# Scores tiles of four heads by 32 queries, one array tile per score matmul, and another order of transfers in layer one

## What is computed

```python
# layer 0: 8 query heads of 64, one key/value head
h = rms(x) * (ln1_w * (1 + cond @ tw.T));  q, k, v = h @ Wq.T, h @ Wk.T, h @ Wv.T   # q, k rotated by position
x = x + (softmax(q @ k.T / 8) @ v) @ Wo.T
h = rms(x) * (ln2_w * (1 + cond @ tw2.T));  x = x + (silu(h @ Wg.T) * (h @ Wu.T)) @ Wd.T   # 2048 inner features
# layer 1: 16 query heads of 32, 4 key/value heads from a latent of 128
y = layernorm(x) * (1 + scale(cond)) + shift(cond)
q, k, v = y @ Wq.T, (y @ Wkd.T) @ Wku.T, (y @ Wkd.T) @ Wvu.T                        # q, k rotated
out = x + (softmax(q @ k.T / sqrt(32)) @ v) @ Wo.T
```

## Time and profile before

| | |
|---|---|
| median of 3 runs | 859.61 us (858.96 to 860.92) |
| the profiled execution | 855.91 us |
| its span, first to last instruction | 854.1 us |
| TensorE matmul busy | 834.2 us, 98% |
| TensorE weight load busy | 685.0 us, 80% |
| VectorE, ScalarE, GpSimd busy | 596.8, 442.7, 404.5 us |
| TensorE's granted clock | 1.000 of full speed |

### The profile page before, as it was taken

One profiled execution on the slowest core, in us unless ns is written; L12 is line 12 of the kernel. 1 busy time (PEld: TensorE's weight loads), 2 busy tenths in 40 slices (PEclk: granted clock), 3 DMA queues, 4 the chain that ended last, 5 costly groups with the idle time before them and its releaser, 6 DMA issues.

```text
span 854.1 us, 15629 instructions
## 1 busy us (share of the span) xinstructions
PE 834.2 (98%) x5940; PEld 685.0 (80%) x5940; DVE 596.8 (70%) x877; ACT 442.7 (52%) x819; POOL 404.5 (47%) x318
## 2 busy tenths in 40 slices
PE   9899999999999999999999999999999999999997
PEld 6687788788788788787787888887878878887885
DVE  6787466666665765766556787876867857668886
ACT  4666455455345455444447556465364454544662
POOL 2566545545544445446455646354444443531431
DMA  9902533533533533523623546446255254240001
GB/s 347 365 25 75 167 115 102 179 121 108 179 102 102 179 103 114 164 82 126 211 103 118 164 143 187 142 150 189 91 164 159 96 167 163 79 130 14 26 27 38
DMA packets 114298, 113.54 MB, mean 133 GB/s; under 512 B 57520, under 2 KB 80048, under 8 KB 114224
## 3 DMA queue, kind: packets, MB, share of 16 engines
q1 hardware_dynamic: 113504, 112.45, 41.1%
q10 hardware_dynamic: 720, 0.09, 0.1%
HBM read 88.15 MB, written 24.38 MB: 132 GB/s over the span
## 4 chain that ended last, share of the span: by engine, by line
PE 75%; issue 6%; DVE 5%; DMA 5%; POOL 4%; ACT 3%; SPq 1%; POOLq 0%; ACTq 0%; DVEq 0%
PE ps L703 24%; PE ps L705 22%; PE ps L704 22%; DMA turned_q<-tq 1%; DVE ex L1441 1%; DMA wost<-WoT 1%; PE ps L972 1%; PE ps L794 1%; PE ps L740 1%; DMA turned_y<-txy 1%; PE ps L822 1%; ACT yf L1871 1%; DMA qkT<-turned_q 1%; POOL wol L629 1%; DVE u L1405 1%
## 5 line engine op out<-in xcount | busy, mean ns | idle before, releaser
L703 PE MATMUL ps<-h2h,guh 128*128 128x512 f32 x512 | 203.5, 397 | 2.2 <-issue 1.2
L705 PE MATMUL ps<-h2l,guh 128*128 128x512 f32 x512 | 199.7, 390 | 0.0
L704 PE MATMUL ps<-h2h,gul 128*128 128x512 f32 x512 | 199.6, 390 | 0.0
L568 POOL TENSOR_TENSOR gul<-rgu,guh 128x1024 fp32r<-128x1024 f32 x64 | 161.2, 2518 | 69.8 <-ACT guh L1779 69.7
L573 POOL TENSOR_TENSOR wdl<-rwd,wdh 128x512 fp32r<-128x512 f32 x64 | 83.0, 1296 | 139.6 <-ACT wdh L1787 139.6
L1340 DVE TENSOR_TENSOR xres<-ps,xres 128x512 f32<-128x512 f32 x128 | 87.6, 685 | 59.2 <-PE ps L705 58.6
L703 PEld LDWEIGHTS ps<-h2h,guh 128*128 128x128 f32 x512 | 96.0, 188 | 28.6 <-issue 9.0
L705 PEld LDWEIGHTS ps<-h2l,guh 128*128 128x128 f32 x512 | 96.1, 188 | 21.0
L704 PEld LDWEIGHTS ps<-h2h,gul 128*128 128x128 f32 x512 | 96.2, 188 | 19.0
L703 PE MATMUL ps<-wdh,ah 128*128 128x512 f32 x256 | 100.3, 392 | 2.6 <-DVE al L1335 1.4
L704 PE MATMUL ps<-wdh,al 128*128 128x512 f32 x256 | 99.7, 389 | 0.0
(11 more groups left out here) (179 smaller groups left out, 1639.5 us busy)
## 6 DMA issues: line engine op xcount, KB each, us to landing
rgu<-gu SPq DMA_DIRECT2D x64, 512.0 KB, 4.7
rwd<-WdT SPq DMA_DIRECT2D x64, 256.0 KB, 4.1
turned_q<-tq SPq DMA_DIRECT2D x20, 320.0 KB, 2.4
qkT<-turned_q SPq DMA_DIRECT2D x20, 320.0 KB, 3.7
turned_p<-tp SPq DMA_DIRECT2D x9, 512.0 KB, 2.6
pT<-turned_p SPq DMA_DIRECT2D x9, 512.0 KB, 3.9
xt<-xT SPq DMA_DIRECT2D x16, 256.0 KB, 3.5
out<-xres SPq DMA_DIRECT2D x15, 256.0 KB, 3.6
```

Source lines behind the costliest of these rows:

```text
L568: pool.tensor_tensor(gul[i][:, :], rgu[i][:, :], guh[i][:, :], ALU.subtract).then_inc(m_gul, 1)
L703: pe.matmul(dst, lh, rh, start=start, stop=False)
L704: pe.matmul(dst, ll, rh, start=False, stop=False)
L705: return pe.matmul(dst, lh, rl, start=False, stop=stop)
```

## The change

It has four parts. First, in both layers a score matmul now holds four heads of 32 queries (128 columns: `qkT` is laid out in four "words" of 32 tokens, each with its heads side by side) where it held 64 queries of one head, so there are 8 of them a tile in layer 0 and 16 in layer 1, each over the full width of the array. Softmax rows are then four heads by 32 queries. The queries come back from DRAM by `back`, in runs of 640 bytes, where `back_in_rows` read runs of 128 bytes. Second, contexts: the values are one plain tile (`v0`, `v1`) copied by one instruction; context is four quarter-array matmuls in all steps of layer 0, and 8 with 256 columns in layer 1. Third, tables and order in layer one: FILL1 at u = -1 and 0; SyncE's order in a step; y is scaled and shifted on ScalarE, and its low part made on GpSimd, after the f4 pieces; on VectorE two pieces come ahead of the rotation in step 9. Fourth, at s = 15 ScalarE's norm1(0) stands behind the f1 pieces, VectorE's turn_y(0) and SyncE's y_away(0) behind the f2 pieces.

```diff
-FILL1 = {-1: (4, 4, 0, 4, 0), **{u: (4, 2, 2, 2, 2) for u in range(0, 9)}, 9: (0, 0, 0, 0, 0)}
+FILL1 = {-1: (4, 2, 2, 2, 2), 0: (4, 2, 4, 2, 0), **{u: (4, 2, 2, 2, 2) for u in range(1, 9)}}
...
-            qkT = sb("qkT", [P, KT + 1, P], into=l0)
+            qkT = sb("qkT", [P, W, KT + 1, B32], into=l0)
...
+        def of_all(ap):
+            return ap.rearrange("p k f -> p (k f)")
...
             def queries_back1(t):
...
-                back_in_rows(qkT1, dq1[t, :, :], ld_q1)
+                back(qkT1, dq1[t, :, :], ld_q1)
...
                 if 0 <= u < TAIL:
                     probs_away1(u)
-                if u < TAIL:
-                    y_away(u + 2)
-                if 0 <= u < TAIL:
                     probs_back1(u)
                 if u < TAIL:
+                    queries_away1(u + 1)
+                    y_away(u + 2)
+                    queries_back1(u + 1)
                     y_back(u + 2)
-                fill(pieces, f2)
-                if u < TAIL:
-                    queries_away1(u + 1)
-                    queries_back1(u + 1)
+                fill(pieces, f2 + f3 + f4 + f5)
                 if u > 0:
                     store(u - 1)
-                fill(pieces, f3 + f4 + f5)
...
             def scores(t):
...
-                for j in range(KT):
+                for h in range(2):
                     for b in range(2):
                         for i in range(2):
-                            r, q = slice(HD0 * i, HD0 * (i + 1)), slice(S * b, S * (b + 1))
-                            mm = pe.matmul(ps[q, XB[2 + rows_of(t, b, i)], S * j:S * (j + 1)], qkT[r, j, q],
-                                           qkT[r, KT, q], start=True, stop=True)
+                            r, n = slice(HD0 * i, HD0 * (i + 1)), 2 * h + b
+                            mm = pe.matmul(ps[:, XB[2 + i], S * n:S * (n + 1)], of_all(qkT[r, 2 * b + h, 0:KT, :]),
+                                           qkT[r, 2 * b:2 * b + 2, KT, :], start=True, stop=True, tile_position=(HD0 * i, 0))
...
             def context(t):
...
-                    mm = pe.matmul(ps[:, BG, 256 * b:256 * (b + 1)], bdv[t % 2][:, b, :],
-                                   pT[:, 2 * b:2 * b + 2, :, :], start=True, stop=True)
+                    for i in range(2):
+                        r = slice(S * b, S * (b + 1))
+                        mm = pe.matmul(ps[HD0 * i:HD0 * (i + 1), ctx_bank(t, b), 0:256], v0[t % 2][r, :],
+                                       pT[r, :, 2 * i:2 * i + 2, :],
+                                       start=True, stop=True, tile_position=(S * b, HD0 * i))
...
             def scores1(t):
...
-                for g in range(4):
+                for h in range(2):
                     for b in range(2):
                         for j in range(KT):
-                            r, q = slice(HD1 * j, HD1 * (j + 1)), slice(S * b, S * (b + 1))
-                            mm = pe.matmul(ps[q, banks1(t)[j], S * g:S * (g + 1)], qkT1[r, g, q], qkT1[r, KT, q],
-                                           start=True, stop=True, tile_position=(HD1 * j, S * b))
+                            r, n = slice(HD1 * j, HD1 * (j + 1)), 2 * h + b
+                            if t < NT - 1:
+                                q, k = of_all(qkT1[r, 2 * b + h, 0:KT, :]), qkT1[r, 2 * b:2 * b + 2, KT, :]
+                            else:
+                                q, k = last_queries(b)[r, 2 * S * h:2 * S * (h + 1)], last_keys(b)[r, :]
+                            mm = pe.matmul(ps[:, banks1(t)[j], S * n:S * (n + 1)], q, k, start=True, stop=True,
+                                           tile_position=(HD1 * j, 0))
...
             def context1(t):
...
-                    for r in range(2):
-                        for j in range(KT):
-                            rows, heads = slice(S * r, S * (r + 1)), pT1[S * r:S * (r + 1), :, 2 * j:2 * j + 2, :]
-                            to = ctx_view1(banks1(t)[2 + r])[HD1 * j:HD1 * (j + 1), :, 2 * b:2 * b + 2, :]
-                            mm = pe.matmul(to, v1[t % 2][rows, b, j, :],
-                                           heads[:, 2 * b:2 * b + 2].rearrange("p w i f -> p i w f"),
-                                           start=True, stop=True, tile_position=(S * r, HD1 * j))
+                    for j in range(KT):
+                        r = slice(S * b, S * (b + 1))
+                        mm = pe.matmul(ps[HD1 * j:HD1 * (j + 1), banks1(t)[2 + b], 0:256], v1[t % 2][r, j, :],
+                                       pT1[r, :, 2 * j:2 * j + 2, :],
+                                       start=True, stop=True, tile_position=(S * b, HD1 * j))
...
             def values1(t):
...
-                for b in range(2):
-                    for i in range(2):
-                        ins = act.copy(v1[t % 2][S * i:S * (i + 1), b, :, :].rearrange("p (c j) d -> p c j d", c=2),
-                                       ps[S * b:S * (b + 1), at:at + 2, QQ1 + KK1:QK1]
-                                       .rearrange("p c (j d) -> p c j d", j=2))
-                ins.then_inc(b_v, 1)
+                act.copy(v1[t % 2][:, :, :].rearrange("p (c j) d -> p c j d", c=2),
+                         ps[:, at:at + 2, QQ1 + KK1:QK1].rearrange("p c (j d) -> p c j d", j=2)).then_inc(b_v, 1)
...
-                if u < TAIL:
-                    scale_shift_y(u + 2)
-                    high_y(u + 2)
                 fill(pieces, f4)
                 if ready is not None:
                     high_h2(ready)
                 if soon is not None:
                     norm2(soon)
+                if u < TAIL:
+                    scale_shift_y(u + 2)
+                    high_y(u + 2)
```

More of the change, by code:

```diff
@@ L156, in build @@
         qkr1 = sb("qkr1", [P, D + P])
-        v1 = [sb(f"v1_{i}", [P, 2, KT, HD1]) for i in range(2)]
-        sb("pad2", [P, 4 * KT * HD1])
-        qkT1 = sb("qkT1", [P, KT + 1, P])
+        v1 = [sb(f"v1_{i}", [P, KT, HD1]) for i in range(2)]
+        sb("pad2", [P, 6 * KT * HD1])
+        qkT1 = sb("qkT1", [P, W, KT + 1, B32])
         ex1 = sb("ex1", [P, KT, 4, S])
@@ L220, in in_words, with by_word @@
             return ap.rearrange("p k (w f) -> p k w f", w=W)
+        def by_word(ap):
+            return ap.rearrange("p (w f) -> p w f", w=W)
         def by_entry(ap):
@@ L233, in downs_before, with ctx_bank, from_entries, entries @@
             return TPB * ((n - RING) // 2 + 1) if n >= RING else 0
[L235 to L249, removed]
+        def ctx_bank(t, b):
+            return (BG, BU)[b] if t <= HEAD else XB[2 + b]
+        def from_entries(at, k):
+            return ps[:, at:at + 2, 0:S * k].rearrange("p b (j q) -> p b j q", j=k)
+        def entries(ap):
+            return ap.rearrange("p j (b q) -> p b j q", b=2)
+        def of_all(ap):
+            return ap.rearrange("p k f -> p (k f)")
+        def last_queries(b):
+            return qkT1[:, :, :, :].rearrange("p w k f -> p (w k f)")[:, D // 2 * b:D // 2 * (b + 1)]
+        def last_keys(b):
+            return qkT1[:, :, :, :].rearrange("p w k f -> p (w k f)")[:, D + S * b:D + S * (b + 1)]
         def x2_bank(t):
@@ L815, in context @@
                     wait(pe, a_cl, t)
+                    wait(pe, a_gf, t - 1)
                 else:
@@ L1033, in context_last @@
                 for b in range(2):
-                    for r in range(2):
-                        for j in range(KT):
-                            rows = slice(S * r, S * (r + 1))
-                            mm = pe.matmul(ps[HD1 * j:HD1 * (j + 1), last_ctx(h) + r, S * b:S * (b + 1)],
-                                           v1[t % 2][rows, b, j, :], pT1[rows, 2 * b:2 * b + 2, 2 * j + h, :],
-                                           start=True, stop=True, tile_position=(S * r, HD1 * j))
+                    for j in range(KT):
+                        r = slice(S * b, S * (b + 1))
+                        mm = pe.matmul(ps[HD1 * j:HD1 * (j + 1), last_ctx(h) + b, 0:P], v1[t % 2][r, j, :],
+                                       pT1[r, :, 2 * j + h, :], start=True, stop=True,
+                                       tile_position=(S * b, HD1 * j))
                 mm.then_inc(b_ctx, 1)
@@ L1478, in low_ctx1 @@
                 wait(dve, b_wo, t)
-                dve.tensor_tensor(by_pair(ycl[:, :, :]), both(t), by_pair(yc[:, :, :]),
+                dve.tensor_tensor(entries(ycl[:, :, :]), from_entries(banks1(t)[2], KT), entries(yc[:, :, :]),
                                   ALU.subtract).then_inc(b_cl, 1)
@@ L1611, in _ @@
                     turn_probs1(u)
+                if u == TAIL:
+                    fill(pieces, 2)
                 if in_layer(u + 1):
@@ L1614, in _ @@
                 if u == TAIL:
-                    fill(pieces, 2)
                     probs_T1(u)
@@ L1910, in high_ctx1 @@
                 wait(act, b_wo, t)
-                act.copy(by_pair(yc[:, :, :]), both(t)).then_inc(b_ch, 1)
```

(3 more changed lines are left out.)

98 lines of the change are left out of this document (41 added, 57 removed).

## The result

The changed kernel takes 864.42 us (median of 10, 861.53 to 865.96), the kernel before, run beside it, 858.94 us (median of 10, 856.13 to 861.99). The ratio is 1.0064 with a 95% interval of 1.0046 to 1.0082: slower by 5.5 us, where 3.8 us were forecast. The profiled execution is one of 864.20 us with a span of 862.4. Two of the later executions, one of the kernel with y ahead of f4 (1651 us, still counted in its median of 855.40) and one of the kernel before (2102 us), are left out of the ratios.

The account below looks back on a forecast made before the run. The prediction took TensorE to bound the kernel nearly everywhere. Its terms, 5.0 + 3.7 - 5.2 + 0.3 = +3.8 us, added to 859.6 gave 863.4 us, with a range of 856.5 to 868.5 (8 times in 10).

Parts of the forecast that it names:

- Scores, layer 0: Score matmuls of layer 0, steps 5 to 15: each group 0.45 us longer, 11 x 0.45 = +5.0 us.
- this end: Score groups of both layers: the load of 128 columns bounds each round, so a group takes 1.07 us.
- Scores, layer 1: Score matmuls of layer 1: each group 0.23 us longer than 0.84, 16 x 0.23 = +3.7 us.
- rivals by hidden loads: Score rounds of both layers: loads don't bound them, groups take 0.62 us, total 849.0 us; chance 0.15.
- by the number of instructions: Score matmuls: cost goes by the instruction count, halved groups take about 0.31 and 0.42 us, total 840.8 us; chance 0.04.
- The first five steps: Layer 0's first five steps: +0.45 us each for scores, -0.45 each for the context in quarters; nothing remains.
- The waits removed: TensorE's waits where the change reorders work (queries, al, down result, silu, probabilities) all go: -5.2 us together.
- the table's row at -1, step 15 and step 9: Layer one's earlier query turning, silu ahead of norm1(0), down results before rotation: waits of 1.3, 1.0 and 1.1 us go.
- al in step 6: Layer one: TensorE's 1.4 us wait on al goes, as SyncE has no weight load ahead of the queries.
- New waits: Layer one, steps 0 and 8: y's work after f4 comes later, counted at +0.3 us for both.
- the third rival: TensorE's waits stay or change places: nothing of the 5.2 us is won, 868.3 us; chance 0.17.
- the prediction's own sign: Wrong if score pairs start 0.06 us apart, or layer one's TensorE idle between 402 and 780 us isn't below 2 us.

Follow-up runs that it names:

- the kernel with y ahead of f4: Changed kernel with score matmuls cut in two, plus y's ScalarE and GpSimd work back ahead of the f4 pieces in layer one: 855.40 us, ratio 0.9951.
- Score halves: Changed kernel with each score matmul cut into two that hold 64 columns each: 855.73 us, ratio 0.9961.
- double moving: Changed kernel with half of its score matmuls moving 128 key columns instead of 64: 863.77 us, ratio 1.0044.
- old shapes, best order: Kernel before, own shapes, with only the table's row at -1, step 15 and step 9 of the new order: 855.65 us, ratio 0.9961.
- each edit alone: On the changed kernel with score matmuls cut in two, layer one: y ahead of f4 alone, 855.40 us; SyncE's old order alone, 856.14 us.
- both together: Changed kernel with score matmuls cut in two, plus SyncE's old order and y ahead of f4 in layer one: 852.31 us, ratio 0.9912.
- The kernel with one weight load first: Changed kernel with SyncE issuing the f2 pieces' gate weight load ahead of the queries' way out in layer one's step 0: 863.66 us, ratio 1.0051.
- The old shapes with the new order: Kernel before, shapes untouched, with all of the new order (table, SyncE, ScalarE, GpSimd, VectorE, step 15): 855.57 us, ratio 0.9972.

## Why the prediction was right

**Scores, layer 0: +5.0, measured 0.41 a group.** The term's mechanism and size hold: 11 x 0.41 = 4.5 us. The step 8 x 0.11 + 0.054 + 0.14 was 0.03 high for a group. Score halves and double moving show it from both sides: 64 columns held give 0.62 us back, 128 moving add nothing. The pairs start 0.11 us apart, as was forecast. The reason given for this end, one load under way at a time on a tile, does not hold by the records: on one tile loads of 188 ns start 0.112 us apart, and in the old group loads of 131 ns start 0.058 apart. What bounds a round is the spacing of the loads, not the length of their records.

**Scores, layer 1: +3.7, measured 16 x 0.21 = 3.3 us.** Right. The rivals by hidden loads and by the number of instructions are out. The surplus of 0.22 us that the prediction couldn't price does go with the number of records: it is gone with 32 (1.05 us beside layer 0's 1.04) and back with 64 in score halves (0.84). In both traces with 64 records the first four rounds of eight start 0.06 us apart, and the other 32 records start one after another in 0.40 us, where four more rounds would take 0.23; why is open. That the load goes by its columns and that 32 rows take as long as 128, as the Trainium skill has it ("TensorE: Matmul & The Clock Gate", LDWEIGHTS), the trace bears out with 187 ns for 32 rows and 188 for 64 or 128, and with rounds 0.112 us apart for 128 columns and 0.058 for 64. By the 107 ns that the prediction estimates from the Trainium skill its sum would have been some 0.6 us smaller (27 groups of 8 rounds, 3 ns each), not 0.4. The cost for each matmul whatever its columns ("TensorEngine Tiling (Array Packing)" in the Trainium skill, instruction overhead), taken as one that adds up over the array tiles, the trace does not bear out: half the instructions took longer.

**The first five steps: nothing, measured +1.1 us.** This step failed. I took the context's -0.45 in full: of what runs beside the context I had weighed x2_T and project, and not ScalarE's copy of the queries, for which the scores now wait 0.34 us. The first wait for the MLP's first piece fell from 1.2 to 0.7 us in return, which is in the next row of the ledger.

**The waits removed: -5.2, all five gone.** Right by place. The mechanisms named for the table's row at -1, step 15 and step 9 were tried only together (old shapes, best order: the waits of 1.0, 1.3 and 1.1 us are not in its trace). The waits gave more than their own length: with al's wait of 1.4 us the step from u = 7 to 8 took 35.15 us, 1.72 more than the 33.43 of its neighbours. Of the 0.28 us above the wait 0.11 are the load of the first matmul behind it, which nothing hides, and some 0.16 are the last matmul ahead of it, which takes 0.39 us where the next would else start 0.23 us behind it. For al in step 6 I named SyncE's order; but with SyncE's old order that wait comes back neither with the new shapes nor with the old ones (old shapes, best order). What removes it stays open; the kernel before has one trace, so it may be that execution's alone.

**New waits: +0.3, measured 1.3 + 1.9 + 0.7 = 3.9 us.** This is the term that was wrong, by more than the 1.5 us that the forecast gave the waits to either side, and it is the third rival inside the forecast: that what is next in line comes as late. "The weights stand ahead of the store" was read as a gain, while the same edit puts them behind the queries' and y's ways out and back; and y's 3.4 us ahead of step 1's exp, which I named at the price of a rival, I counted at next to nothing. The first two waits are in every trace with the changed order and shapes; the 0.7 us of step 8 stand in the changed kernel's alone and may be that execution's. By the prediction's own sign this part was wrong: between 402 and 780 us TensorE's idle time was to be below 2 us, and it is 4.3.

```profile
402.00:780.00 378.00, 373.69 (x2090) 307.76 (x2089) 269.85 (x358) 191.90 (x327) 181.73 (x126) 1.00 0.43 140
```

That the sum came near the result is in part luck: this error and the first steps' (+4.7 us together) were partly met by scores 0.9 us cheaper and by waits that gave back more than they lasted.

**The profile's time and the median.** The 3.7 us between the profiled execution and the median were added as they stood. They are most likely the clock: 1.000 in that execution and 0.992 to 0.998 in most timed runs of the kernel before. Where in the span a timed run lost it is not recorded; of the 13 profiled executions ten ran part of the last step at half clock, four a piece behind a wait in the middle, and three a piece around 30 us.

## What to carry to other kernels

Price a small matmul as a round on its array tile, by the larger of the columns held and the columns moved: fewer instructions that hold twice the columns cost more wherever the moving side is the shorter. When an instruction is shortened that ran beside a copy, price the copy, and when a queue's item is moved ahead of one thing, list everything that it is now behind. Test two suspected waits both apart and together: here each edit alone left 3.6 us of waits or more, and both together left 1.3.

## What was not expected of the hardware

**A wait of 2 us can cost 3.** Behind some waits in the middle of the kernel TensorE's granted clock fell to 0.50, from 2.4 to 1.2 GHz, and was back about 3 us later. The kernel with one weight load first, in windows behind its wait of 2.0 us, which ended at 525.4 (granted clock behind POOL's column):

```profile
515.00:523.00 8.00, 8.00 (x37) 6.62 (x36) 7.97 (x9) 0.86 (x2) 2.38 (x3) 1.00 0.21 77
525.40:528.40 3.00, 3.00 (x22) 2.11 (x23) 2.19 (x3) 1.64 (x4) 2.39 (x2) 0.60 0.59 194
```

The old shapes with the best order show the same behind 1.8 us, which ended at 485.2:

```profile
480.00:490.00 10.00, 8.23 (x59) 6.19 (x59) 6.55 (x10) 5.74 (x15) 5.91 (x5) 0.83 0.64 216
```

There seven full-array matmuls start 0.427 us apart, not 0.227: 1.4 us more than the wait itself, 1.6 with the two at the edges. The old shapes with the new order (behind 2.1 us) and y ahead of f4 (behind 3.6 us) show it too. The changed kernel's wait of 1.9 us and the 2.4 us of the score halves had no such fall, so a wait this long can cost it and need not. Whether it took part in the 2.5 us by which the kernel with one weight load first missed its expected 861.2 is not shown: its timed runs have mean clocks of 0.994 to 0.998, like the changed kernel's, and most of the miss is the probabilities' wait that stayed.
